# Normalising each score tile in the same step as its maximum, and two fills moved

## The chip, the cores and the metric

The kernel runs on one core of a Trainium2 chip. The metric is device microseconds of one execution. The engines of the core are named as in the profile: PE is TensorE (PEld its weight loads), DVE is VectorE, ACT is ScalarE, POOL is GpSimd and SP is SyncE, which issues most transfers. Every engine runs its own list of instructions in the order in which the program wrote them, and engines wait for each other only through semaphores.

## The reference

The input is `x` of shape (4, 512, 256) and a context of shape (4, 512, 512). Four blocks follow each other, each added to `x` with a gate:

```
x = x + tanh(g_xattn[0]) * L0_xattn(layernorm(x), ctx)   # 16 heads, 1024 keys
x = x + tanh(g_ffn[0])   * L0_ffn(layernorm(x))
x = x + tanh(g_xattn[1]) * L1_xattn(layernorm(x), ctx)   # 16 heads of 64, 512 keys + 1 null key
x = x + tanh(g_ffn[1])   * L1_ffn(layernorm(x))          # 8 experts, top 2
```

The change is in the third block. For each batch and each head it computes, in float32,

```
sim  = (q * scale) @ k.T          # k has a null key in front of its 512 keys
attn = softmax(sim); out = attn @ v
out  = layernorm(out @ Wout) * ln_scale + ln_bias
```

The fourth block starts with a router (logits of 8 experts, the best two, their softmax), whose work for the first batches is interleaved with the third block.

## The kernel before, in words

`layer1` computes the third block. It walks over 32 groups: group `i` is one batch `b` (0 to 3) and one pair of heads `p` (0 to 7), `b, p = divmod(i, 8)`. A group has four steps, `r` = 0 to 3, written out by hand for each engine. The work is staged by one group: in step `r` of group `i`, the scores of query tile `r` (128 queries, two heads of 512 keys, one PSUM bank each) are made for group `i + 1`, while for group `i` the probabilities of key tile `r` are transposed and multiplied with the values.

What each engine writes for a step is this.

- PE: `scores(i + 1, r)` into one of two sets of two banks (so it waits until the exponentials of two tiles ago are done, semaphore `exp_done`), the fill at `(i, r, 0)`, in step 2 the second half of the key projection, `transpose_probs(i, r)` (step 0 waits for `p_ready`, that all four tiles of group `i` are normalised; the others wait for `pT_ready`, that ACT has copied the tile transposed before), the fill at `(i, r, 1)`, and `weigh_values` of the key tile before.
- ACT: `exponentials(i + 1, r)` (two exponentials with a sum each), the read of the fill at `(i, r, 0)`, `keep_probs(i, r)` (the copy of the transposed probabilities), the read of the fill at `(i, r, 1)`, in step 0 `keep_result`, and router work.
- DVE: `maxima(i + 1, r)` (row maximum L1911 and its negative L1913), in step 2 the read of the key projection (L1966), `normalize` (L1919, L1921 and two L1925), `extra` (layer norms and router work at fixed places, a list in `extra`), and its reads of fills.

A fill is some other PE work that uses the one PSUM bank `MISC`: the query projection of group `i + 2` at `(i, 0, 0)`, its key projection at `(i, 1, 0)`, value projections, transposed tokens (`xT`), the null key's scores, the output projection, and the router's transposes (`rT`), `logits` and `prefix` (counts of the chosen experts). The dictionary `slots` gives each its place `(i, r, y)`, with `y` = 0 ahead of the transposes and 1 behind them. Because all share one bank, each fill waits until the one before it has been read, by ACT (`misc_act`) or, for `k`, `null`, `logits`, `prefix` and the second half of `xT`, by DVE (`misc_dve`).

In the kernel before, DVE normalises one step late: in step `r` it normalises tile `r - 1`, and in step 3 tiles 2 and 3.

## Time and profile before

| | us |
|---|---|
| median of 3 executions | 1899.43 (1893.98 to 1903.69) |
| the profiled execution, its own time | 1893.98 |
| its span, first to last instruction | 1892.2 |
| PE busy | 1758.5 (93%) |
| DVE busy | 1215.5 (64%) |
| ACT busy | 1116.9 (59%) |
| POOL busy | 460.0 (24%) |
| mean granted PE clock | 0.986 of full speed |

The span is cut by the program's blocks: the first two blocks of the reference run up to 680 us, `layer1` from 680 to 1447 us, and the experts from there to the end. The shares of busy time are means over these stages. A time in the rows below is counted from the span's start.

### The profile page before, as it was taken

The numbers are of one execution on the slowest core, as the hardware profiler recorded it, in microseconds if no ns is written. First come the engines' busy times: TensorE is split into PE (matmuls) and PEld (weight loads), VectorE is DVE, ScalarE is ACT, GpSimd is POOL, SyncE is SP. The second block draws the span as 40 slices with busy tenths as digits, with TensorE's granted clock in tenths as the row PEclk, the third lists the DMA queues.
The fourth block names the chain that finished last, engine by engine and source line by source line (L and its number), as shares of the span: only waits on it lengthen the run. The fifth ranks groups of instructions, "written<-read, shape, count | busy, mean of one in ns | idle before, by whom it ended". The sixth has DMA issues, their size and how long they took to land. (4 is left out here: it accounts for less than half of the span.)

```text
span 1892.2 us, 28143 instructions
## 1 busy us (share of the span) xinstructions
PE 1758.5 (93%) x9516; PEld 1109.3 (59%) x9516; DVE 1215.5 (64%) x2860; ACT 1116.9 (59%) x2332; POOL 460.0 (24%) x434
## 2 busy tenths in 40 slices
PE   5899997998899999999999999999988989999997
PEld 3555554555454444444544454445436989999997
DVE  4877776876777565455456455645755886666664
ACT  2466666666667556555455545554553666776674
POOL 3010110110110110000010002000204587777775
PEclk9899999999999999999999999999998999999999
DMA  3000000010003066000000000100007568667760
GB/s 101 1 23 1 1 23 1 1 29 0 1 1 134 1 207 200 22 1 1 1 9 15 1 1 24 34 1 12 18 7 245 159 197 229 191 194 223 197 197 6
DMA packets 123054, 128.12 MB, mean 68 GB/s; under 512 B 10912, under 2 KB 118304, under 8 KB 122912
## 3 DMA queue, kind: packets, MB, share of 16 engines
q1 hardware_dynamic: 114176, 117.65, 19.8%
q0 software_dynamic: 8160, 8.67, 2.5%
q8 instruction: 77, 1.26, 0.3%
q14 instruction: 65, 0.53, 0.1%
q10 hardware_dynamic: 576, 0.00, 0.0%
HBM read 97.43 MB, written 30.69 MB: 68 GB/s over the span
## 5 line engine op out<-in xcount | busy, mean ns | idle before, releaser
L1155 DVE TENSOR_REDUCE l_tile_max<-psum 128x1 f32<-128x512 f32 x512 | 342.0, 688 | 105.8 <-PE psum L833 104.3
L1911 DVE TENSOR_REDUCE l_row_max<-psum 128x2 f32<-128x1024 f32 x124 | 151.8, 1224 | 254.1 <-PE psum L1566 253.5
L1003 ACT ACTIVATE l_probs<-psum 128x1024 f32<-128x1024 f32 x256 | 248.2, 1021 | 106.8 <-PE psum L845 103.3
L2578 POOL TENSOR_TENSOR moe_w_lo<-moe_w,moe_w_hi 128x512 fp32r<-128x512 f32 x184 | 259.5, 1411 | 116.9 <-ACT moe_w_hi L2360 115.2
L833 PE MATMUL psum<-l_kT,l_qT 128*128 128x512 f32 x512 | 237.1, 471 | 40.5 <-DVE l_tile_max L1155 37.2
L1752 ACT ACTIVATE l_null_p<-l_s_null,l_neg_max 128x1 f32<-128x1 f32 x248 | 71.6, 289 | 276.9 <-DVE l_neg_max L1913 273.6
L2290 PE MATMUL psum<-moe_xs_hi,moe_w_hi 128*128 128x256 f32 x736 | 212.1, 288 | 2.0 <-DVE moe_xs_lo L2410 2.0
L2290 PE MATMUL psum<-moe_xs_lo,moe_w_hi 128*128 128x256 f32 x736 | 209.7, 285 | 0.0
L2290 PE MATMUL psum<-moe_xs_hi,moe_w_lo 128*128 128x256 f32 x736 | 209.5, 285 | 0.0
L833 PEld LDWEIGHTS psum<-l_kT,l_qT 128*128 128x128 f32 x512 | 98.1, 192 | 131.6 <-DVE l_tile_max L1155 111.1
L1754 ACT ACTIVATE l_probs<-psum,l_neg_max 128x512 f32<-128x512 f32 x248 | 166.6, 672 | 0.0
L845 PE MATMUL psum<-l_qT,l_kT 128*128 128x512 f32 x512 | 161.3, 399 | 1.5 <-ACT l_probs L1003 1.5
L1697 PEld LDWEIGHTS psum<-ident,l_probs 128*128 128x128 f32 x1024 | 119.7, 142 | 71.2 <-issue 59.4
L2558 DVE TENSOR_TENSOR psum<-psum,moe_gate 128x256 f32<-128x256 f32 x184 | 78.8, 428 | 112.9 <-ACT moe_gate L2390 112.8
L2390 ACT ACTIVATE moe_gate<-psum 128x256 f32<-128x256 f32 x184 | 70.9, 385 | 135.6 <-PE psum L2290 134.9
L2290 PEld LDWEIGHTS psum<-moe_xs_hi,moe_w_hi 128*128 128x128 f32 x736 | 142.8, 194 | 2.2 <-DVE moe_xs_lo L2410 2.2
L2290 PEld LDWEIGHTS psum<-moe_xs_lo,moe_w_hi 128*128 128x128 f32 x736 | 142.9, 194 | 0.0
L2290 PEld LDWEIGHTS psum<-moe_xs_hi,moe_w_lo 128*128 128x128 f32 x736 | 142.7, 194 | 0.0
L1566 PE MATMUL psum<-l_qk 64*128 64x512 f32 x496 | 140.9, 645 | 1.2 <-PEq L774 1.2
L860 PE MATMUL psum<-l_probs,l_v_ones 128*32 128x512 f32 x1024 | 139.0, 615 | 0.6 <-ACT l_probs L1003 0.6
L1711 PE MATMUL psum<-l_probsT,l_v_sb 128*64 128x512 f32 x512 | 139.1, 622 | 0.0
L1697 PE MATMUL psum<-ident,l_probs 128*128 128x128 f32 x1024 | 134.7, 275 | 4.2 <-DVE l_probs L1925 3.0
(323 smaller groups left out, 3284.8 us busy)
## 6 DMA issues: line engine op xcount, KB each, us to landing
moe_w<-in_moe_w SPq DMA_DIRECT2D x276, 256.0 KB, 4.7
moe_sorted_x<-l_zeros SPq DMA_DIRECT2D x1, 17680.0 KB, 56.1
moe_xs<-moe_sorted_x SPq DMA_DIRECT2D x23, 272.0 KB
moe_w<-in_ctx SPq DMA_DIRECT2D x8, 512.0 KB, 3.5
moe_w<-in_ctxT SPq DMA_DIRECT2D x4, 1024.0 KB, 5.8
moe_w<-in_wkv SPq DMA_DIRECT2D x2, 2048.0 KB, 15.5
x_resid<-in_x SPq DMA_DIRECT2D x4, 512.0 KB, 10.1
out_x<-x_resid SPq DMA_DIRECT2D x4, 512.0 KB
```

What stands on the lines that cost most here:

```text
L833: nc.tensor.matmul(bank(max_bank(m)), qT[:, q % SLOTS, h, t * P:(t + 1) * P], kT[:, q % SLOTS, h // 2, half * BANK:(half + 1) * BANK], sta ...
L845: last = nc.tensor.matmul(bank(2 * (n % 2) + i), kT[:, q % SLOTS, c, kt * P:(kt + 1) * P], qT[:, q % SLOTS, 2 * c + i, :], start=True, sto ...
L860: last = nc.tensor.matmul(bank(O_BANK)[32 * j:32 * j + 32, :], v_ones[:, q % SLOTS, kt, j, :], probs[:, (n + j // 2) % PT_RING, j % 2, :], ...
L1003: nc.scalar.activation(probs[:, n % PT_RING], wide(2 * (n % 2)), ACT.Exp, scale=SCALE).then_inc(exp_done, 1)
L1155: nc.vector.reduce_max(tile_max[:, q % 2, t, h, half:half + 1], bank(max_bank(m)), AX_X).then_inc(max_read, 1)
L1566: last = nc.tensor.matmul(bank(2 * (t % 2) + j), q_sb[head, i % 2, t * P:(t + 1) * P], k_sb[head, i % 2, :], start=True, stop=True)
L1697: last = nc.tensor.transpose(bank(4 + j)[:, t * P:(t + 1) * P], probs[i % 2][:, t, j, kt * P:(kt + 1) * P], ident[:])
L1711: last = nc.tensor.matmul(bank(O_BANK)[j * DH:(j + 1) * DH, :], v_sb[:, kt, h * DH:(h + 1) * DH], probsT[:, m % 2, j, :], start=(kt == 0), ...
L1754: last = nc.scalar.activation(probs[i % 2][:, t, j, :], bank(2 * (t % 2) + j), ACT.Exp, bias=neg_max[:, t, j:j + 1], scale=SCALE, accum_ou ...
L1911: nc.vector.reduce_max(row_max[:, t, :], wide(2 * (t % 2)).rearrange("p (j m) -> p j m", j=2), AX_X)
L2290: last = nc.tensor.matmul(up_bank(k)[:, n * ROWS:(n + 1) * ROWS], w, x_part[:, i % 2, c, :], start=(c == 0 and j == 0), stop=(c == s.DC - ...
L2578: nc.gpsimd.tensor_tensor(w13_lo[:, k % SPLITS], w13[:, slot_k, :, cols], w13_hi[:, k % SPLITS].bitcast(F32), ALU.subtract).then_inc(w13_s ...
```

## The change

```diff
@@ slots, for batch b + 1 < 4, pair p == 5
-            slots.update({(i, 2, 1): ("xT", b + 1, 0), (i, 3, 0): ("xT", b + 1, 1)})
+            slots.update({(i, 2, 1): ("xT", b + 1, 0), (i, 3, 1): ("xT", b + 1, 1)})
@@ slots of the router, for the routed batches c = 0 and 1
-            at = (first, 2, 1), (first + 1, 0, 1), (first + 2, 2, 1), (first + 4, 0, 1)
+            at = (first, 2, 1), (first + 1, 0, 1), (first + 2, 2, 1), (first + 4, 2, 1)
@@ DVE's step
                         if r == 2:
                             read_fill((i, 1, 0))
-                        if i + 1 < GROUPS and r >= 1:
-                            normalize(i + 1, r - 1)
                         extra(*divmod(i, PAIRS), r)
-                        if i + 1 < GROUPS and r == 3:
+                        if i + 1 < GROUPS:
                             normalize(i + 1, r)
                         if r != 1:
                             read_fill((i, r, 0))
                         read_fill((i, r, 1))
```

There are three edits. DVE now normalises tile `r` in step `r`, behind `extra` and ahead of its reads of fills. The second half of the transposed tokens (`xT`, pair 5 of batches 0 to 2) goes from ahead of the transposes of step 3 to behind them. The router's `prefix` of the first two routed batches (pair 3 of batches 2 and 3) goes from step 0 to step 2. Apart from the order and the waits that hang on it, the instructions are the same. Lines of the changed kernel behind this place are two lower (L2290 is L2288).

On DVE, a plain pair of heads early in the block (batch 0, pair 0, steps 2 and 3) had these rows before, where `l_denom`, `l_recip` and `l_probs` are `normalize` and `l_row_max`, `l_neg_max` are `maxima`:

```order
L1911 TENSOR_REDUCE l_row_max<-psum 128x2 [waits l1_s_psum]
L1913 SCALAR_TENSOR_TENSOR l_neg_max<-l_row_max,l_s_null 128x2
L1919 TENSOR_TENSOR l_denom<-l_p_sum,l_null_p 128x2 [waits l1_exp_done]
L1921 RECIPROCAL l_recip<-l_denom 128x2
L1925 TENSOR_SCALAR l_probs<-l_probs,l_recip 128x512 x2
L1919 TENSOR_TENSOR l_denom<-l_p_sum,l_null_p 128x2 [waits l1_exp_done]
L1921 RECIPROCAL l_recip<-l_denom 128x2
L1925 TENSOR_SCALAR l_probs<-l_probs,l_recip 128x512 x2
L1911 TENSOR_REDUCE l_row_max<-psum 128x2 [waits l1_s_psum]
L1913 SCALAR_TENSOR_TENSOR l_neg_max<-l_row_max,l_s_null 128x2
```

and now has these:

```order
L1911 TENSOR_REDUCE l_row_max<-psum 128x2 [waits l1_s_psum]
L1913 SCALAR_TENSOR_TENSOR l_neg_max<-l_row_max,l_s_null 128x2
L1919 TENSOR_TENSOR l_denom<-l_p_sum,l_null_p 128x2 [waits l1_exp_done]
L1921 RECIPROCAL l_recip<-l_denom 128x2
L1925 TENSOR_SCALAR l_probs<-l_probs,l_recip 128x512 x2
L1911 TENSOR_REDUCE l_row_max<-psum 128x2 [waits l1_s_psum]
L1913 SCALAR_TENSOR_TENSOR l_neg_max<-l_row_max,l_s_null 128x2
```

The pattern of maxima and normalisation is now the same in all four steps, and the wait for `exp_done` ahead of the next `maxima` is for the tile whose maximum was just taken.

On PE, at pair 3 of batch 3, step 2 had these rows before (`l_qk` scores, L1582 the key projection, L1697 the transposes, L1711 the values, L1588 the value projection of step 3), with the `prefix` ahead of all of them in step 0:

```order
L1566 MATMUL psum<-l_qk 128x512 [waits l1_exp_done]
L1582 MATMUL psum<-moe_w 128x512 x2
L1697 MATMUL psum<-ident,l_probs 128x128 [waits l1_pT_ready]
L1711 MATMUL psum<-l_probsT,l_v_sb 64x512 [waits l1_pT_ready]
L1566 MATMUL psum<-l_qk 128x512 [waits l1_exp_done]
L1588 MATMUL psum<-moe_w 128x512 [waits l1_misc_read_dve]
```

and now, with only the first row of each kind shown as above:

```order
L1566 MATMUL psum<-l_qk 128x512 [waits l1_exp_done]
L1582 MATMUL psum<-moe_w 128x512 x2
L1697 MATMUL psum<-ident,l_probs 128x128 [waits l1_pT_ready]
L1645 MATMUL psum<-router_either,router_lower 128x32 [waits l1_zeroed,l1_either_ready,l1_misc_read_dve]
L1646 MATMUL psum<-router_either,router_ones 128x32
L1711 MATMUL psum<-l_probsT,l_v_sb 64x512 [waits l1_pT_ready]
L1566 MATMUL psum<-l_qk 128x512 [waits l1_exp_done]
L1588 MATMUL psum<-moe_w 128x512 [waits l1_misc_read_dve]
```

The `prefix` (L1645, L1646) stands right ahead of the value projection L1588, one block of scores and values between them, and L1588 now waits for DVE's read of the `prefix`; before, that wait was for the read of the keys.

On DVE, at pair 6 of batch 3 (steps 0 and 1, `router_either` the end of the expert ranking) the rows before were:

```order
L498 TENSOR_SCALAR router_either<-router_rank 128x32
L1911 TENSOR_REDUCE l_row_max<-psum 128x2 [waits l1_s_psum]
L1913 SCALAR_TENSOR_TENSOR l_neg_max<-l_row_max,l_s_null 128x2
L1919 TENSOR_TENSOR l_denom<-l_p_sum,l_null_p 128x2 [waits l1_exp_done]
L1921 RECIPROCAL l_recip<-l_denom 128x2
L1925 TENSOR_SCALAR l_probs<-l_probs,l_recip 128x512 x2
L502 TENSOR_TENSOR router_work<-router_chosen,router_logits 128x32
```

and now are:

```order
L498 TENSOR_SCALAR router_either<-router_rank 128x32
L1919 TENSOR_TENSOR l_denom<-l_p_sum,l_null_p 128x2 [waits l1_exp_done]
L1921 RECIPROCAL l_recip<-l_denom 128x2
L1925 TENSOR_SCALAR l_probs<-l_probs,l_recip 128x512 x2
L1911 TENSOR_REDUCE l_row_max<-psum 128x2 [waits l1_s_psum]
L1913 SCALAR_TENSOR_TENSOR l_neg_max<-l_row_max,l_s_null 128x2
L502 TENSOR_TENSOR router_work<-router_chosen,router_logits 128x32
```

The normalisation of tile 0 stands ahead of the maximum of tile 1.

## Rows read from the trace of the kernel before

**Rows 1.** layer1: us; busy of PE, PEld, DVE, ACT, POOL; PEclk, DMA share, GB/s.

```profile
680.00:1447.00 767.00, 742.28 (x3092) 359.31 (x3092) 415.30 (x1137) 411.98 (x1015) 48.96 (x72) 0.99 0.14 44
```

**Rows 2.** Waits of PE, then of DVE: total us, times, longest us.

```profile
PE psum L1573 <- DVE l_rows L1968: 6.7, 3, 2.4
PE psum L1645 <- ACT l_qk L1769: 2.2, 2, 1.1
...
DVE l_row_max L1911 <- PE psum L1566: 253.5, 106, 6.4
DVE l_denom L1919 <- ACT l_probs L1754: 12.2, 20, 0.6
```

**Rows 3.** Timeline, batch 0, pairs 2 to 3: start us, duration us, engine, line.

```profile
733.74 1.13 PE L1566 MATMUL psum<-l_qk 64*128 64x512 f32 x4
736.83 1.13 PE L1566 MATMUL psum<-l_qk 64*128 64x512 f32 x4
741.70 1.13 PE L1566 MATMUL psum<-l_qk 64*128 64x512 f32 x4
...
734.91 1.22 DVE L1911 TENSOR_REDUCE l_row_max<-psum 128x2 f32<-128x1024 f32 x1 [0.99 <-PE psum L1566]
738.03 0.19 ACT L1754 ACTIVATION_READ_ACCUMULATOR l_probs<-psum,l_neg_max 128x1 f32 x1
738.25 0.16 DVE L1919 TENSOR_TENSOR l_denom<-l_p_sum,l_null_p 128x2 f32<-128x2 f32 x1 [0.61 <-ACT l_probs L1754]
739.53 1.22 DVE L1911 TENSOR_REDUCE l_row_max<-psum 128x2 f32<-128x1024 f32 x1
```

**Rows 4.** Timeline of batch 3, pair 3, steps 0 and 2 to 3.

```profile
1327.74 0.41 PE L1645 MATMUL psum<-router_either,router_lower 128*128 128x32 f32 x2 [1.11 <-ACT l_qk L1769]
1328.31 1.08 PE L1711 MATMUL psum<-l_probsT,l_v_sb 128*64 128x512 f32 x4
1328.48 0.87 DVE L521 TENSOR_TENSOR router_run<-router_run,psum 128x8 f32<-128x8 f32 x4 [1.63 <-PE psum L1646]
1337.86 0.15 DVE L1919 TENSOR_TENSOR l_denom<-l_p_sum,l_null_p 128x2 f32<-128x2 f32 x1
1339.30 0.16 DVE L86 TENSOR_TENSOR l_out_work<-l_out_work 128x4 f32<-128x4 f32 x1
1340.09 3.70 PE L1588 MATMUL psum<-moe_w 128*128 128x512 f32 x8
1342.10 1.22 DVE L1911 TENSOR_REDUCE l_row_max<-psum 128x2 f32<-128x1024 f32 x1
1345.93 1.56 PE L1588 MATMUL psum<-moe_w 128*128 128x512 f32 x3 [1.27 <-ACT l_v_sb L1774]
```

**Rows 5.** Timeline, query projections behind the tokens' second half: batches 1 and 2.

```profile
1000.18 1.98 PE L1573 MATMUL psum<-l_rows,moe_w 128*128 128x512 f32 x4 [2.44 <-DVE l_rows L1968]
...
1195.03 0.19 ACT L1754 ACTIVATION_READ_ACCUMULATOR l_probs<-psum,l_neg_max 128x1 f32 x1
1195.83 0.15 DVE L1919 TENSOR_TENSOR l_denom<-l_p_sum,l_null_p 128x2 f32<-128x2 f32 x1
1197.84 3.48 PE L1573 MATMUL psum<-l_rows,moe_w 128*128 128x512 f32 x4 [2.44 <-DVE l_rows L1968]
```

**Rows 6.** PE in stretches around waits: us, PE busy, PEclk, DMA share, GB/s.

```profile
1198.00:1202.00 4.00, 4.00 (x12) 0.64 0.02 4
1002.00:1006.00 4.00, 4.00 (x19) 1.00 0.00 0
```

**Rows 7.** Timeline of batch 3, pair 6, the last exponentials.

```profile
1405.56 1.22 DVE L1911 TENSOR_REDUCE l_row_max<-psum 128x2 f32<-128x1024 f32 x1
1409.82 1.09 PE L1697 MATMUL psum<-ident,l_probs 128*128 128x128 f32 x8 [0.50 <-ACT l_probsT L1792]
1417.15 0.19 ACT L1754 ACTIVATION_READ_ACCUMULATOR l_probs<-psum,l_neg_max 128x1 f32 x1
1418.79 1.48 PE L1697 MATMUL psum<-ident,l_probs 128*128 128x128 f32 x8 [3.04 <-DVE l_probs L1925]
```

## The prediction

> **What bounds the kernel now.** I read the stages first, then each engine's waits, then the timeline at the places where PE waits. In layer1, from 680 to 1447 us, PE is busy 742.3 of 767.0 us at 0.99 of its full clock [rows 1], so the block can give at most 25 us whatever DVE does, and less, since some of those 25 us hang on other things. DVE is busy 415 us of it. Then the waits: PE's for DVE and ACT are short and few; the ones that the change touches are 6.7 us in three waits for DVE's read of the transposed tokens (L1968), 2.2 us in two waits ahead of the prefix [rows 2], and 3.04 us once, near the end, for the normalised probabilities [rows 7]. DVE for its part waits 253.5 us in 106 waits for PE's scores, and only 12.2 us in 20 waits for the exponentials [rows 2]. So PE paces the block, and DVE's order matters only where it makes PE late.
>
> **Edit 1, normalising in the same step: the ring.** It removes no instruction. It makes DVE wait for the exponentials of tile r before it may take the maximum of tile r+1, in steps 0 to 2 of 31 groups (93 waits that were covered by the step's delay). Queued behind each wait are the four instructions of the normalisation, DVE's reads of fills at steps 0, 2 and 3, and the next maximum; ACT waits for that maximum, and behind ACT's exponentials stand its copies, for which PE waits. This makes a ring: maximum, exponentials, normalisation, next maximum. The trace has the ring already, in step 3, where DVE normalised tile 3 at once: the maximum starts at 734.91, ACT's last piece ends at 738.03 + 0.19 = 738.22, DVE goes on at 738.25, and the next maximum starts at 739.53 [rows 3]. That is 4.62 us a turn. PE's step with a query or key projection in it, from one start of the scores to the next, is 741.70 - 736.83 = 4.87 us [rows 3], and most steps of the block are as long or longer, so DVE should wait 0.2 us for the scores in such a step in place of some 2 us, and PE should not notice. The 253.5 us of DVE's wait for scores go mostly to the row for the exponentials. PE is guarded a second time: a late maximum delays PE only through ACT's copy of the transposed tile, and through the scores two tiles on, which come 5 us later.
>
> Where the ring shows all the same is behind a step without a projection (736.83 - 733.74 = 3.1 us [rows 3]), where the maximum was already late: it starts at 739.53, while the scores that started at 736.83 end at 736.83 + 1.13 = 737.96, 1.6 us sooner [rows 3]. There are three such places, all in batch 0: the opening step, pair 0 to 1 and pair 2 to 3. In the opening the second maximum comes 1.2 us late and recovers 0.2 us a step; the copy ahead of the step 3 transposes is then about 0.2 us late. Term: +0.2 us.
>
> Work in extra (layer norm, router) used to come on top of the normalisation and now fits into the wait for the exponentials. DVE gains there, PE does not, save in edit 2.
>
> **Edit 2, the transposed tokens.** The wait for L1968 ends with DVE's normalisation of tile 3, not with PE's transposes, so moving these behind the other transposes should cost and bring nothing by itself. But the normalisation of tile 2 is no longer in that step. In batches 1 and 2 it had pushed that of tile 3 back: DVE began at 1195.83 [rows 5], while the exponentials ended at 1195.03 + 0.19 = 1195.22 [rows 5]. Without it DVE begins at 1195.25. So two of the three waits fall from 2.44 to about 1.87 us, the size of the third (6.7 - 2 x 2.44 = 1.8). Term: -1.15 us.
>
> **Edit 3, the prefix.** It stood behind the query projection in the same bank and waited 1.11 us for ACT, twice [rows 2, 4]; this goes: -2.2 us. In step 2 it follows the key read, which is done. But the value projection L1588 of step 3 then waits until DVE has read the prefix, and DVE reads it behind extra and the new normalisation. In batch 3: DVE is free at 1337.86 (key read done) [rows 4]; the nine small instructions and two scalings of the layer norm took 1339.30 to 1342.10 = 2.8 us [rows 4], so they end at 1340.7; the normalisation takes 739.53 - 738.25 = 1.28 us [rows 3] to 1342.0; the read takes 0.87 + 0.25 us by L521 and the instruction behind it [rows 4], so to 1343.2. PE would reach L1588 at 1340.09 plus the prefix's own 0.57 us (1328.31 - 1327.74) = 1340.66 [rows 4]. It waits about 2.5 us. In batch 2 the two scalings are not in that step: 1.9 us. Against this, the next value projection waited 1.27 us in batch 3 for ACT [rows 4] and 0.62 us in batch 2, since the maximum of step 3 was late (1342.10); with PE itself held back, the late maximum is covered and these waits go. Net: 2.5 + 1.9 - 2.2 - 1.3 - 0.6 = +0.3 us. Bounds: -2.2 us if DVE is in time after all, +4.4 us if none of the removed waits counts.
>
> **The last groups.** In pair 6 of batch 3 DVE has router work in every step, and its maxima are late already: step 1's starts at 1405.56, right behind the ranking of experts [rows 7]. There the normalisation now stands ahead of it: 1405.56 + 1.3 = 1406.86. ACT's exponentials end 3.3 us later (738.22 - 734.91 [rows 3]) at 1410.2, its copy at 1411.2, and PE's transposes, which began at 1409.82 after a 0.50 us wait, begin at 1411.2. Step 2's maximum starts at 1411.5, step 3's at 1411.5 + 4.6 = 1416.1. ACT's row scaling still lies between, so the last exponentials end at 1419.4 against 1417.34 [rows 7], and the last normalisation lets PE go at 1420.85 against 1418.79. Term: +2.1 us. The slot numbers and scaled rows for the scatter, and the list with which SP starts the expert weights, follow the same instructions and shift as much, so nothing behind gives it back. Bounds: 0 and +3 us.
>
> **Sum.** 0.2 - 1.15 + 0.3 + 2.1 = +1.5 us on the profiled execution, 1893.98 us (its span is 1892.2). This execution is the fastest of the three; the median is 1899.43, 5.4 us above. I forecast against the median: 1899.4 + 1.5 = 1901 us.
>
> **The clock.** A wait of 2.44 us was followed once by a stretch at 0.64 of the full clock, between the two levels of 1.2 and 2.4 GHz, in which four query matmuls took 3.48 us in place of 1.98, and once, just as long, by none [rows 5, 6]. So each wait of 2 to 3 us is a coin with 1.5 us on it for 2 us of matmuls. Two of them shrink (batch 2's may keep its clock, -1.5), one of 2.5 us is new ahead of 3.70 us of value projection (up to +3.7).
> The Trainium skill, "TensorE: Matmul & The Clock Gate", Part 1, says that the hardware looks at activity in windows that run freely of the program. By that rule the same wait may or may not cost, as here; the trace agrees, with 1.00 behind one wait of 2.44 us and 0.64 behind the other.
>
> **Rivals.**
> - Gain (1897.5 us): the waits for DVE shrink, the slow stretch of batch 2 goes, and the last groups lose nothing because DVE's extra work there covers the wait. 0.2 - 1.15 - 1.5 + 0.3 = -2.1. For it: DVE has fewer instructions in step 3. Against: in the last groups DVE's start row [rows 7] shows no idle time to give.
> - Slower, the ring longer than PE's step: if a turn costs 5.3 us in place of 4.62, each step of 4.87 us loses 0.43, three in a row 1.3. Of this 0.4 us is slack: ACT's copy takes about 1.1 us behind its exponentials, so it ends 3.3 + 1.1 = 4.4 us after the maximum starts, and PE's transposes of step 3, where no fill stands ahead of them, come 4.87 - 1.17 + 1.1 = 4.8 us after it (1.17 from the scores' start to the maximum: 734.91 - 733.74 [rows 3]). In the dozen groups without that fill PE loses 0.9 us each, +11 us, 1911 us. It decides from a turn of about 5.2 us (0.8 us a group). For it: no step 0 to 2 of the trace shows the ring closed, and the margin is 0.2 us. Against: 20 waits in step 3 all look alike (12.2 / 20 = 0.61 us) [rows 2], with 0.03 us from ACT's end to DVE's start.
> The Trainium skill, same page, "Architectural detail", says that ScalarE and VectorE take their queues strictly in order. By it a waiting normalisation holds the next maximum even where the scores are ready; the trace agrees: DVE waits until 738.25, and the maximum of scores that ended at 737.96 starts at 739.53. It is this rival's reason, and the 0.2 us are its margin.
> - Clock (1905 us): the new wait ahead of the value projection is followed by a slow stretch, 1.5 + 3.7 = +5.2 us.
> - The last groups' 2.1 us double, since ACT is held by the row scaling too: +3.6, 1903 us; inside the range.
>
> **Chances.** Forecast within 2 us of its sum 0.58, gain 0.14, clock and last groups 0.16, ring 0.12. About 0.5%, 9.5 us, is what a measurement of this kernel can tell from no change. Only the ring reaches it, and run noise (the three times spread over 9.7 us): faster 0.04, same 0.85, slower 0.11. The range reaches from the gain to the threshold: 1895 to 1909 us.
>
> **What would show it.** Right: DVE's wait for scores falls from 253 us to well under 100, and that for the exponentials rises from 12 to over 100; the steps of 4.87 us stay; L1573's three waits are all near 1.9 us; L1645's ACT wait is gone and L1588 waits for DVE about 2 us twice; the transposes of the last pair start some 2 us later. Wrong: PE waits for copies (L1697 for ACT) in ordinary groups, which is the ring, or a step with a projection longer than 4.87 us where no PE wait stood before.

## The result and the profile after

| | before | after |
|---|---|---|
| median beside each other (8 runs each) | 1900.35 us | 1911.67 us (1900.76 to 1917.78) |
| ratio, 95% interval | | 1.0055 [1.003, 1.0082] |
| span of the profiled execution | 1892.2 us | 1904.4 us |
| mean granted PE clock | 0.986 | 0.983 |

The changed kernel is slower by 0.55%, and its median lies above the range of 1895 to 1909 us. Compared twice more on later occasions it gave 1.0019 [1.0002, 1.0037] and 1.0028 [1.0011, 1.0045]. The three together are about 1.0034, that is +6.5 us. So the cost is real; the later two put it at +3.6 and +5.3 us, the first at +10.5 us.

The two profiled executions differ by 12.2 us of span. To divide that, I cut both at two marks: the first scores of layer1 (L1566), and the last pair's transposes (L1697, the row with the wait of about 3 us for the probabilities [rows 7]). The stretch between them is called layer1's stretch below.

| us | before | after | difference |
|---|---|---|---|
| up to the first scores | 680.23 | 685.96 | +5.7 |
| layer1's stretch | 738.56 | 744.37 | +5.8 |
| from there to the end | 473.4 | 474.1 | +0.7 |

The first 5.7 us lie in code that the change doesn't touch. In other profiled executions of the same changed kernel the first scores start at 681.45 and 685.87 us. So the 5.7 us are not the change's. Its own cost is layer1's stretch: +5.8 us. In two further executions of the changed kernel the same stretch grew by 6.3 and 8.6 us (e10 and e5 below), so one execution's stretch holds to some 3 us; what the change costs is therefore read place by place.

What answers to [rows 1] is this stretch of the changed kernel, with the same columns:

```profile
686.00:1459.00 773.00, 745.14 (x3092) 360.38 (x3092) 423.04 (x1137) 411.60 (x1015) 48.62 (x72) 0.99 0.14 44
```

PE has the same 3092 instructions; it is busy 2.9 us longer and idle 3.1 us longer (773.00 - 745.14 = 27.9 against 24.7 us). So half of the cost is waits, and half is the same matmuls taking longer.

The waits, to be held against [rows 2]:

```profile
DVE l_row_max L1911 <- PE psum L1566: 136.4, 78, 7.9
DVE l_denom L1919 <- ACT l_probs L1754: 133.6, 103, 1.9
...
PE psum L1573 <- DVE l_rows L1968: 5.6, 3, 1.9
PE psum L1588 <- DVE router_work L524: 5.6, 2, 3.4
PE psum L1697 <- ACT l_probsT L1792: 3.2, 2, 1.8
```

About half of DVE's idle time moved from the scores to the exponentials, and PE hardly notices: there is no new PE wait in ordinary groups. The wait for scores did not fall to "well under 100" us, as the prediction had it, but to 136.4. The block's 123 steps from one block of scores to the next take 731.6 us, 5.95 us on the mean, and a turn of 4.62 us leaves 1.3 us of each. New are the two waits of L1588 for DVE's read of the prefix, 5.6 us together. Two waits for ACT's copies in the last pair but one grew from 1.2 to 3.2 us together.

The plain steps of batch 0, pairs 2 to 3, where [rows 3] stand, read now:

```profile
734.78 1.13 PE L1566 MATMUL psum<-l_qk 64*128 64x512 f32 x4
739.64 1.13 PE L1566 MATMUL psum<-l_qk 64*128 64x512 f32 x4
742.73 1.13 PE L1566 MATMUL psum<-l_qk 64*128 64x512 f32 x4
...
740.81 1.22 DVE L1911 TENSOR_REDUCE l_row_max<-psum 128x2 f32<-128x1024 f32 x1 [0.16 <-PE psum L1566]
744.15 0.16 DVE L1919 TENSOR_TENSOR l_denom<-l_p_sum,l_null_p 128x2 f32<-128x2 f32 x1 [1.88 <-ACT l_probs L1754]
745.43 1.22 DVE L1911 TENSOR_REDUCE l_row_max<-psum 128x2 f32<-128x1024 f32 x1
```

Here the ring is closed in every step. A turn is 745.43 - 740.81 = 4.62 us, PE's step with a projection is still 739.64 - 734.78 = 4.86 us, and DVE waits just 0.16 us for scores. A step without projection (3.09 us) makes the next maximum late, and PE loses nothing.

The place of the prefix in batch 3, to be held against [rows 4]:

```profile
1341.36 0.16 DVE L86 TENSOR_TENSOR l_out_work<-l_out_work 128x4 f32<-128x4 f32 x1
1343.50 0.73 DVE L154 TENSOR_SCALAR l_rows<-l_rows,l_out_mv,l_out_work 128x256 f32<-128x256 f32 x2
1343.99 1.50 POOL L1853 TENSOR_TENSOR l_rows<-l_rows,l_ln_scale 128x256 f32<-128x256 f32 x2 [150.06 <-DVE l_rows L154]
1344.15 0.68 DVE L1919 TENSOR_TENSOR l_denom<-l_p_sum,l_null_p 128x2 f32<-128x2 f32 x1
1345.15 1.02 DVE L1925 TENSOR_SCALAR l_probs<-l_probs,l_recip 128x512 f32<-128x512 f32 x2
1346.27 0.88 DVE L521 TENSOR_TENSOR router_run<-router_run,psum 128x8 f32<-128x8 f32 x4
1347.22 0.19 DVE L524 TENSOR_TENSOR router_work<-router_run,psum 128x32 f32<-128x32 f32 x1
1347.46 6.55 PE L1588 MATMUL psum<-moe_w 128*128 128x512 f32 x8 [3.44 <-DVE router_work L524]
```

DVE has no idle moment from the layer norm to the read at 1347.22. PE waits 3.44 us, and then its eight value matmuls take 6.55 us where they took 3.70 [rows 4]. The stretches of this place (the two of batch 2 first) show why. Columns are us, then busy of PE, PEld, DVE, ACT and POOL, then PEclk:

```profile
1147.00:1151.00 4.00, 3.72 (x6) 1.68 (x7) 2.51 (x8) 1.81 (x6) 1.51 (x2) 0.68 0.00 0
1151.00:1155.00 4.00, 4.00 (x15) 2.14 (x14) 0.83 (x2) 1.62 (x2) 0.00 (x0) 0.90 0.00 0
1347.00:1351.00 4.00, 3.54 (x4) 1.51 (x5) 3.29 (x9) 1.81 (x6) 1.82 (x2) 0.50 0.01 2
1351.00:1355.00 4.00, 4.00 (x14) 2.25 (x13) 1.43 (x4) 0.68 (x2) 0.62 (x3) 0.72 0.00 0
```

The granted clock is 0.50 behind the wait of batch 3, which is the lower level of 1.2 GHz, and 0.68 behind the wait of 2.12 us in batch 2, where the value matmuls take 5.40 us.

Each place of the sum, from one mark to the next in both traces:

| us | forecast | measured |
|---|---|---|
| opening, up to pair 1 | +0.2 | +0.2 |
| transposed tokens, batches 1 and 2 | -1.15 | -0.57 - 2.06 = -2.6 |
| prefix, batches 2 and 3 | +0.3 | +1.88 + 3.69 = +5.6 |
| router's logits, pair 5 of batch 3 | none | +0.6 |
| last pair | +2.1 | 19.50 to 21.50, +2.0 |
| sum | +1.5 | +5.8 of 5.8 |

### The profile page after: what moved, and what is told of

It is laid out like the page before. It is cut to its first block and busy times, and to the rows that moved or that the text cites. A ratio compares the mean times of both kernels' runs of the same rounds, so it can differ in the third digit from the quotient of the medians.

```text
span 1904.4 us, 28143 instructions
## 1 busy us (share of the span) xinstructions
PE 1764.4 (93%) x9516; PEld 1111.8 (58%) x9516; DVE 1223.9 (64%) x2860; ACT 1115.9 (59%) x2332; POOL 459.3 (24%) x434
## 5 line engine op out<-in xcount | busy, mean ns | idle before, releaser
L1911 DVE TENSOR_REDUCE l_row_max<-psum 128x2 f32<-128x1024 f32 x124 | 151.6, 1223 | 137.5 <-PE psum L1566 136.4
L2288 PE MATMUL psum<-moe_xs_hi,moe_w_hi 128*128 128x256 f32 x736 | 211.5, 287 | 1.4 <-DVE moe_xs_lo L2408 1.4
L2288 PE MATMUL psum<-moe_xs_lo,moe_w_hi 128*128 128x256 f32 x736 | 209.2, 284 | 0.0
L2288 PE MATMUL psum<-moe_xs_hi,moe_w_lo 128*128 128x256 f32 x736 | 209.0, 284 | 0.0
L1697 PEld LDWEIGHTS psum<-ident,l_probs 128*128 128x128 f32 x1024 | 119.3, 142 | 75.2 <-issue 59.2
L2288 PEld LDWEIGHTS psum<-moe_xs_hi,moe_w_hi 128*128 128x128 f32 x736 | 142.2, 193 | 1.7 <-DVE moe_xs_lo L2408 1.7
L2288 PEld LDWEIGHTS psum<-moe_xs_lo,moe_w_hi 128*128 128x128 f32 x736 | 142.3, 193 | 0.0
L2288 PEld LDWEIGHTS psum<-moe_xs_hi,moe_w_lo 128*128 128x128 f32 x736 | 142.2, 193 | 0.0
L1566 PE MATMUL psum<-l_qk 64*128 64x512 f32 x496 | 140.9, 645 | 1.2 <-PEq L774 1.2
L1697 PE MATMUL psum<-ident,l_probs 128*128 128x128 f32 x1024 | 134.8, 275 | 6.2 <-ACT l_probsT L1792 3.2
L1711 PE MATMUL psum<-l_probsT,l_v_sb 128*64 128x512 f32 x512 | 139.1, 622 | 0.0
```

The lines of the kernel that those rows point to most:

```text
L1566: last = nc.tensor.matmul(bank(2 * (t % 2) + j), q_sb[head, i % 2, t * P:(t + 1) * P], k_sb[head, i % 2, :], start=True, stop=True)
L1697: last = nc.tensor.transpose(bank(4 + j)[:, t * P:(t + 1) * P], probs[i % 2][:, t, j, kt * P:(kt + 1) * P], ident[:])
L1711: last = nc.tensor.matmul(bank(O_BANK)[j * DH:(j + 1) * DH, :], v_sb[:, kt, h * DH:(h + 1) * DH], probsT[:, m % 2, j, :], start=(kt == 0), ...
L1911: nc.vector.reduce_max(row_max[:, t, :], wide(2 * (t % 2)).rearrange("p (j m) -> p j m", j=2), AX_X)
L2288: last = nc.tensor.matmul(up_bank(k)[:, n * ROWS:(n + 1) * ROWS], w, x_part[:, i % 2, c, :], start=(c == 0 and j == 0), stop=(c == s.DC - ...
```

## Experiments

The table gives, for all twelve, the ratio to the kernel before on the same chip, and layer1's stretch in the profiled execution (before: 738.56 us).

| kernel | ratio [95%] | layer1's stretch |
|---|---|---|
| e1, edit 1 alone | 0.9995 [0.9978, 1.0012] | 741.3 (+2.8) |
| e2, edit 3 alone | 1.0025 [1.001, 1.004] | 742.9 (+4.3) |
| e3, edits 1 and 2 | 0.9999 [0.9981, 1.0017] | 741.5 (+3.0) |
| e4, edit 2 alone | 1.0006 [0.9987, 1.0025] | 738.6 (+0.1) |
| e5, changed kernel again | 1.0019 [1.0002, 1.0037] | 747.1 (+8.6) |
| e6, prefix read first | 1.0013 [0.9996, 1.0029] | 741.8 (+3.2) |
| e7, changed, 2 multiplications more | 1.0338 [1.0318, 1.0357] | 804.5 (+65.9) |
| e8, before, 2 multiplications more | 1.0112 [1.0093, 1.013] | 761.9 (+23.4) |
| e9, edits 1 and 2, last pair but one in the old order | 1.0013 [0.9996, 1.0031] | 739.5 (+1.0) |
| e10, changed kernel a third time | 1.0028 [1.0011, 1.0045] | 744.8 (+6.3) |
| e11, changed, GpSimd's multiplication small | one execution | 744.8 (+6.2) |
| e12, changed, 1 multiplication more | 1.0146 [1.012, 1.0173] | 766.2 (+27.6) |

### One edit at a time

e1 has the new order of `normalize` alone:

```diff
-                        if i + 1 < GROUPS and r >= 1:
-                            normalize(i + 1, r - 1)
                         extra(*divmod(i, PAIRS), r)
-                        if i + 1 < GROUPS and r == 3:
+                        if i + 1 < GROUPS:
                             normalize(i + 1, r)
```

> Edit 1 alone: DVE normalises each tile in its own step; both fills stay where they were. Theory A (the step-by-step account: the ring of 4.62 us fits into PE's steps, only the last groups are late): PE's steps of 4.86 us stay, the transposes of the last pair come 2 us later, the token waits shrink to 1.87 us, no wait of L1588 for DVE; layer1 about +1 us, time between -2 and +3 us of before. Theory B (the ring is what made the changed kernel slower by 11 us): the whole loss is here, +8 to +12 us.

e2 has the move of the prefix alone:

```diff
-            at = (first, 2, 1), (first + 1, 0, 1), (first + 2, 2, 1), (first + 4, 0, 1)
+            at = (first, 2, 1), (first + 1, 0, 1), (first + 2, 2, 1), (first + 4, 2, 1)
```

> Edit 3 alone, with the old order of the normalisation: the router's prefix in step 2 of pair 3. Theory A (the prefix is late because of the layer norm work in front of DVE's read of it, and each wait is followed by slow matmuls): L1588 waits 2.1 and about 3 us for DVE, both followed by value projections of 5.4 to 6.5 us in place of 3.7; +5 to +6 us. Theory B (the new normalisation, which waits for the exponentials, is what holds the read back): no wait over 1 us here, -2 us.

e3 is the changed kernel with that line put back:

```diff
-            at = (first, 2, 1), (first + 1, 0, 1), (first + 2, 2, 1), (first + 4, 2, 1)
+            at = (first, 2, 1), (first + 1, 0, 1), (first + 2, 2, 1), (first + 4, 0, 1)
```

> The changed kernel without edit 3 (prefix back in step 0; edits 1 and 2 stay). Theory A: the two long waits of L1588 and their slow stretches are gone, the waits of 1.1 us of L1645 are back, the last groups still 2 us late: about 5.6 us faster than the changed kernel, 0 to +2 us against before. Theory B (ring): as slow as the changed kernel, +9 to +11 us.

e4 has the move of the tokens' second half alone:

```diff
-            slots.update({(i, 2, 1): ("xT", b + 1, 0), (i, 3, 0): ("xT", b + 1, 1)})
+            slots.update({(i, 2, 1): ("xT", b + 1, 0), (i, 3, 1): ("xT", b + 1, 1)})
```

> Edit 2 alone: the second half of the transposed tokens behind the transposes of step 3, old order of the normalisation. Theory A: nothing depends on it, waits of L1573 stay 1.9, 2.4 and 2.4 us, 0 us within 2 us. Rival: the move alone gives the gain of the token waits, -1 to -3 us.

Only the move of the prefix is outside no change by its interval: 1.0025 alone, and without it the rest is 0.9999. In e2's trace L1588 waits for DVE 2.00 us in batch 2 and 2.77 us in batch 3, and both times the value matmuls behind it took 5.40 us. The stretches of batch 3 show the clock. Their columns are us, PE busy, PEclk, DMA share, GB/s:

```profile
1341.00:1345.00 4.00, 1.23 (x7) 1.00 0.00 0
1345.00:1349.00 4.00, 4.00 (x6) 0.57 0.01 2
1349.00:1353.00 4.00, 4.00 (x17) 1.00 0.00 0
```

Here the prefix waits with the old order of normalising in place. So its cost comes from where the prefix stands, behind `extra` on DVE, and not only from the new order. The waits give 2.00 + 2.77 less the removed 1.11 + 1.11 + 0.62 + 1.27 = +0.7 us, the slow matmuls 2 x 1.70 = +3.4 us; together 4.1 us. From mark to mark the two places grow by 1.8 us each, 3.6 of the +4.3 us of the stretch, a little under the 5 to 6 us that I expected.

In e3 I expected the stretch to be 5.6 us shorter than the changed kernel's. It is 2.9 us shorter. The two places of the prefix give back 4.9 us, since L1588's wait for ACT in batch 3 is 1.95 us there; but the query projection behind the tokens of batch 2 is slow again, 3.38 us where the changed kernel has 1.98.

e1 and e4 separate the tokens. With edit 2 alone the three waits are 1.88, 2.45 and 2.44 us, as before. With edit 1 alone they are 1.87 us each. The shortening belongs to edit 1, by the mechanism that the prediction gave; edit 2 by itself does nothing. What the clock does behind that wait in batch 2 hangs on edit 3 as well. The changed kernel first, then e1:

```profile
1204.40 1.98 PE L1573 MATMUL psum<-l_rows,moe_w 128*128 128x512 f32 x4 [1.87 <-DVE l_rows L1968]
1198.16 3.22 PE L1573 MATMUL psum<-l_rows,moe_w 128*128 128x512 f32 x4 [1.87 <-DVE l_rows L1968]
```

With the new order and the prefix in step 2 the four matmuls took 1.98 us in all five executions (the changed kernel three times, e6, e11); with the prefix in step 0 they took 3.22 to 3.38 us in all three (e1, e3, e9), behind the same wait. So edit 3 costs 5.6 us in its own places and gives 1.7 us back here, from mark to mark. Why it does is open.

e1's +2.8 us of the stretch is hardly seen in its time: the interval of 0.9978 to 1.0012 ends at +2.3 us. e1's rows of pair 6 of batch 3 and of the mark behind it show its cost:

```profile
1413.28 1.08 PE L1697 MATMUL psum<-ident,l_probs 128*128 128x128 f32 x6 [1.77 <-ACT l_probsT L1792]
1422.97 1.09 PE L1697 MATMUL psum<-ident,l_probs 128*128 128x128 f32 x8 [2.92 <-DVE l_probs L1925]
```

The wait of 1.77 us was 0.50 us before [rows 7]. It is there in every kernel with the new order in that pair (1.77 in e3, 1.76 in e6), and in none with the old (0.50 in e2 and e4).

### The changed kernel twice more

e5 and e10 are the changed kernel itself.

> The changed kernel once more, beside the same executions of the kernel before as the next three. Theory A (layer1 6 us longer, the rest of the first 11 us is the spread between executions): ratio 1.002 to 1.0045, and both value projections behind the prefix slow again. Theory B (a cost of 11 us that the trace of layer1 does not show): 1.005 or more again.

> The changed kernel once more, on another occasion, since its first two comparisons gave ratios of 1.0055 and 1.0019. If layer1's +5.8 us in the traces is all that the change costs, the ratio is 1.003 (+5 to +6 us), and both earlier intervals are one value measured with more scatter than they say. Rival: the first comparison was the right one and the change costs 10 us: 1.0055.

The ratios are 1.0019 and 1.0028. The first comparison's interval begins at 1.003, so the three meet near +6 us, which is what layer1's stretch gives. The place of the prefix is the same every time; e5, batches 2 and 3:

```profile
1142.73 5.40 PE L1588 MATMUL psum<-moe_w 128*128 128x512 f32 x8 [2.12 <-DVE router_work L524]
1342.88 2.07 PE L1588 MATMUL psum<-moe_w 128*128 128x512 f32 x2 [3.44 <-DVE router_work L524]
```

The waits are equal to 0.01 us in all three executions, and the matmuls behind each are slow: the eight take 5.40 us in batch 2 each time, and 6.60 us in e5 and 6.53 us in e10 in batch 3 (the second row above has the first two of e5's eight). What differs lies elsewhere. e5 has a wait of 2.28 us ahead of a value projection of pair 4 (L1588 for ACT) where the first execution has 0.77 us; ACT itself is idle for 1.41 us ahead of that copy, and the trace names no engine of the core for it. In pair 5 the logits' matmuls (L1639) took 2.75 us in place of 1.92. These two places are the whole difference of 2.8 us. And the experts' part took 478.5 us behind the last mark, against 474.1. I have no cause for any of the three.

### The read ahead of the other work

e6 lets DVE read the prefix ahead of `extra` and `normalize`:

```diff
+                        early = slots.get((i, r, 1), ("",))[0] == "prefix"
+                        if early:
+                            read_fill((i, r, 1))
                         extra(*divmod(i, PAIRS), r)
...
-                        read_fill((i, r, 1))
+                        if not early:
+                            read_fill((i, r, 1))
```

> The changed kernel with DVE's read of the prefix ahead of the layer norm work and the normalisation, in step 2 of pair 3 of batches 2 and 3. Theory A (the read stands behind too much DVE work): L1588 no longer waits for DVE's read of the prefix. But the maximum of step 3 stays as late, so the next value projection waits for ACT instead, 1.3 us in batch 2 and 2.5 us in batch 3; about 1.7 us of waits less, and up to 4.5 us of slow matmuls less if the shorter waits keep the clock: -2 to -6 us against the changed kernel. Rival (the prefix is late on PE itself): waits of L1588 for DVE stay over 1.5 us.

The wait for DVE is gone from L1588, and a wait for ACT stands in its place one projection later. The rows of batch 3, and the stretches around them with busy of PE, PEld, DVE, ACT and POOL ahead of the clock:

```profile
1342.47 3.70 PE L1588 MATMUL psum<-moe_w 128*128 128x512 f32 x8
1346.55 1.21 DVE L1911 TENSOR_REDUCE l_row_max<-psum 128x2 f32<-128x1024 f32 x1
1349.75 0.59 ACT L1774 ACTIVATE l_v_sb<-psum 128x512 f32<-128x512 f32 x1
1350.39 3.70 PE L1588 MATMUL psum<-moe_w 128*128 128x512 f32 x8 [3.34 <-ACT l_v_sb L1774]
```

```profile
1347.00:1351.00 4.00, 0.66 (x3) 0.38 (x3) 3.21 (x9) 2.96 (x8) 2.44 (x4) 1.00 0.01 2
1351.00:1355.00 4.00, 4.00 (x12) 1.26 (x10) 0.80 (x2) 0.85 (x2) 0.00 (x0) 1.00 0.00 0
```

The layer norm and the normalisation take DVE until 1346.55 in any case; the maximum of step 3 is late, ACT's exponentials behind it, and behind those ACT's read of the first value projection (1349.75), on which the second waits. The two waits sum to 2.01 + 3.34 = 5.35 us against 2.12 + 3.44 = 5.56. So reading early moves the wait and doesn't remove it; I had expected waits for ACT of 1.3 and 2.5 us, 1.7 us less in all. In batch 2 the matmuls behind the wait take 5.40 us as before, and the place costs as much as in the changed kernel. But behind the 3.34 us of batch 3 the clock stays at 1.00, and that place costs 2.8 us less from mark to mark, the 2.85 us of its slow value matmuls; the stretch is 744.4 - 741.8 = 2.6 us shorter. This divides the two costs on the chip: nearly the same waits, without one of the slow stretches.

### GpSimd beside the normalisation

e11 reduces GpSimd's multiplication by `ln_scale` to four of 256 columns (the output's scale is left out for the others):

```diff
-                        nc.gpsimd.tensor_tensor(rows[:, t, :], rows[:, t, :], ln_scale[:], ALU.mult).then_inc(scaled, 1)
+                        nc.gpsimd.tensor_tensor(rows[:, t, 0:4], rows[:, t, 0:4], ln_scale[:, 0:4], ALU.mult).then_inc(scaled, 1)
```

> The changed kernel, with GpSimd's multiplication by ln_scale (L1853) reduced to the first four columns of 256 (the output's scale is left out for the rest). If that multiplication beside DVE's normalisation is what made the wait of batch 3 longer than predicted, L1588's wait for DVE there falls from 3.44 us to 2.5 to 2.8, with L1919 at 0.16 us and L1925 at 0.88. Rival: the layer norm's own instructions are longer in the chain than I summed; then it stays at 3.2 to 3.5. The wait of batch 2 stays at 2.12 either way.

```profile
1342.35 0.52 POOL L1853 TENSOR_TENSOR l_rows<-l_rows,l_ln_scale 128x4 f32<-128x4 f32 x2 [150.06 <-DVE l_rows L154]
1342.51 0.15 DVE L1919 TENSOR_TENSOR l_denom<-l_p_sum,l_null_p 128x2 f32<-128x2 f32 x1
1342.98 0.88 DVE L1925 TENSOR_SCALAR l_probs<-l_probs,l_recip 128x512 f32<-128x512 f32 x2
1345.15 2.08 PE L1588 MATMUL psum<-moe_w 128*128 128x512 f32 x2 [2.77 <-DVE router_work L524]
```

The wait falls from 3.44 to 2.77 us, L1919 from 0.68 to 0.15 us and L1925 from 1.02 to 0.88 us (0.53 + 0.14 = 0.67 us, all of the difference). The multiplication is the cause. The other 0.27 us over the forecast's 2.5 stay: the chain of layer norm, normalisation and read as summed was that much short. This place is 2.1 us shorter than in the changed kernel (its eight value matmuls take 5.09 us, not 6.55). The stretch did not get shorter (744.8 us), since pair 4 is 0.9 us longer (a wait of 1.65 us ahead of its value projection) and pair 5 2.1 us longer (the logits' matmuls take 3.55 us, not 1.92). I have no cause for these two; it is one execution.

### How near the ring is

e7 adds two multiplications by 1.0 behind each normalisation in the changed kernel, e8 the same in the kernel before, e12 one of them in the changed kernel:

```diff
+                    dve.drain()
+                    for j in range(2):
+                        part = probs[i % 2][:, t, j, :]
+                        last = nc.vector.tensor_scalar(part, part, 1.0, None, ALU.mult)
```

(e12 has `range(1, 2)` in the second line.)

> The changed kernel with each normalisation followed by a second multiplication of the same tiles by 1.0 (0.9 us more of DVE each, no change of values). Theory A (the ring has 0.25 us to spare): a turn is now 5.5 us against PE's 4.86, PE waits for ACT's copy (L1697) in the groups without a fill ahead of the last transposes, +12 to +25 us against the changed kernel. Rival (PE is far from the ring): less than 5 us.

> The kernel before with the same second multiplication. Theory A: the normalisation is off the ring in steps 0 to 2, where DVE waits over 2 us for scores; only the step without a projection, the token waits and the last groups pay: +5 to +10 us against before, much less than the same addition costs the changed kernel. Rival (DVE's busy time itself counts): as much as in the changed kernel.

> The changed kernel with one more multiplication by 1.0, of one head's probabilities, behind each normalisation. With two of them the ring's turn went from 4.61 to 5.44 us and layer1 lost 0.58 us (5.44 - 4.86) in most of its 124 steps. With one the turn is about 5.03: if the margin is the difference of turn and step, 0.25 us, it loses 0.17 us a step, 15 to 22 us over the changed kernel. Rival: the copy's slack of 0.4 us counts, as the prediction had it (decides at 5.2 us), and it loses under 5 us.

e7, steps behind each other in batch 0:

```profile
743.01 1.22 DVE L1911 TENSOR_REDUCE l_row_max<-psum 128x2 f32<-128x1024 f32 x1
748.46 1.21 DVE L1911 TENSOR_REDUCE l_row_max<-psum 128x2 f32<-128x1024 f32 x1
753.90 1.22 DVE L1911 TENSOR_REDUCE l_row_max<-psum 128x2 f32<-128x1024 f32 x1
747.28 1.09 PE L1697 MATMUL psum<-ident,l_probs 128*128 128x128 f32 x8 [1.54 <-ACT l_probsT L1792]
754.04 1.09 PE L1697 MATMUL psum<-ident,l_probs 128*128 128x128 f32 x8 [1.69 <-DVE l_probs L1929]
```

e12, the same places:

```profile
740.89 1.22 DVE L1911 TENSOR_REDUCE l_row_max<-psum 128x2 f32<-128x1024 f32 x1
746.00 1.22 DVE L1911 TENSOR_REDUCE l_row_max<-psum 128x2 f32<-128x1024 f32 x1
740.05 1.09 PE L1697 MATMUL psum<-ident,l_probs 128*128 128x128 f32 x8 [0.87 <-ACT l_probsT L1792]
746.14 1.09 PE L1697 MATMUL psum<-ident,l_probs 128*128 128x128 f32 x8 [1.02 <-DVE l_probs L1929]
```

A turn is 5.44 us in e7 and 5.11 us in e12; there is no idle time ahead of a maximum, and PE waits for ACT's copies in plain groups, which is what the prediction named as the sign of the ring. The stretch grows over the changed kernel's 744.4 us by 60.1 us at a turn of 5.44 and by 21.8 us at 5.11.

Not all of that is the ring: the tokens, the prefix and pairs 4 to 7 of batch 3 grow too. Without these places, counted from one block of scores to the next, e7 loses 40.6 us, in 29 steps that are over 0.4 us longer than the changed kernel's, and e12 12.4 us, in 14 such steps. An estimate from these two: the line through them reaches zero at a turn of 5.11 - 12.4 x 0.33 / 28.2 = 4.96 us, just above PE's step of 4.86.

My expectation of e7 (12 to 25 us) was far too low. The loss stands in one or two steps of a group, as I had it, but not only in groups without a fill: PE also waits for ACT's read of a fill (L1588 for ACT, 12.8 us in seven waits in e7), and a single step loses up to 3.2 us. The expectation of e12 (15 to 22 us at a turn of 5.03) held partly by luck: the turn was 5.11, and a loss in most of 124 steps, as it says, did not occur.

In e8 the same work costs 23.4 us, also above the 5 to 10 us that I expected: in step 3 two normalisations stand in a row, so each place where PE waits for the last of them grows: the tokens' waits of batches 1 and 2 from 2.44 to 4.79 us, the last pair's from 3.04 to 5.54, and two plain groups wait 0.77 us where there was no wait. Both long ones of the tokens were followed by query matmuls of 3.78 us, where the kernel before has 1.98 and 3.48. Outside the places named above e8 loses 4.9 us, against e7's 40.6: that difference is what the new order makes of the same work.

### A version without both losses

e9 puts the prefix back into step 0 and gives the last pair but one the old order of DVE:

```diff
-            at = (first, 2, 1), (first + 1, 0, 1), (first + 2, 2, 1), (first + 4, 2, 1)
+            at = (first, 2, 1), (first + 1, 0, 1), (first + 2, 2, 1), (first + 4, 0, 1)
...
+                        late = i == GROUPS - 2
+                        if late and r >= 1:
+                            normalize(i + 1, r - 1)
                         extra(*divmod(i, PAIRS), r)
-                        if i + 1 < GROUPS:
+                        if i + 1 < GROUPS and (not late or r == 3):
                             normalize(i + 1, r)
```

> The changed kernel with the prefix back in step 0 and, for the last pair but one alone, DVE's old order of normalising. What is left is the shorter wait for the transposed tokens. If the loss sits in the prefix place (+5.6 us in the profile) and in the last groups (+2 us), both are gone: L1588 waits for ACT about 1.3 us in batch 3 and not for DVE, the last pair's transposes wait about 3.0 us as in the kernel before, and layer1 takes 738.6 - 0.6 = about 738 us against 738.56. Time: 0 to -3 us against the kernel before. Rival: the same-step order costs something of its own everywhere; then it stays 2 us or more above.

Both losses are gone in its trace: no wait of L1588 for DVE, and the last pair's transposes as before. What remains is a wait for ACT in batch 3 that was 1.27 us [rows 4]:

```profile
1349.97 3.70 PE L1588 MATMUL psum<-moe_w 128*128 128x512 f32 x8 [1.95 <-ACT l_v_sb L1774]
```

It is 0.7 us longer, as in e1 and e3 (1.95 each), since DVE's maximum stands behind layer norm and normalisation there. From mark to mark the tokens give 0.9 us, while this wait takes 0.7, pair 4 0.3, pairs 5 and 6 0.9 and the opening 0.2 us. The stretch is 739.5 us, +1.0 and not the -0.6 us that I expected; the time is 1.0013 [0.9996, 1.0031]: no change, and no gain over the kernel before. By its time alone the rival, +2 us or more, is not excluded.

## Why the prediction was wrong

The mechanism of each step was as predicted, and one term was mis-sized: **edit 3, the prefix**, "Net: 2.5 + 1.9 - 2.2 - 1.3 - 0.6 = +0.3 us". It measured +5.6 us.

- **The removed waits** went as said: 1.11 twice, 0.62 and 1.27 us.
- **The new waits** were 3.44 and 2.12 us in place of 2.5 and 1.9, +1.2 us. 0.67 us of it is GpSimd's multiplication beside the normalisation (e11). The kernel before had shown this in the same batch, in a normalisation that started beside that multiplication; I read the durations of quiet places and did not look at what runs on GpSimd just then. Its rows:

```profile
1345.22 2.20 POOL L1853 TENSOR_TENSOR l_rows<-l_rows,l_ln_scale 128x256 f32<-128x256 f32 x2 [1.77 <-DVE l_rows L154]
1346.05 0.70 DVE L1919 TENSOR_TENSOR l_denom<-l_p_sum,l_null_p 128x2 f32<-128x2 f32 x1
```

- **The clock** was the larger part. The prediction called the slow stretch behind a wait a coin, gave it nothing in the sum, and put it in a rival of its own, "1.5 + 3.7 = +5.2 us". It cost 1.70 us behind the wait of batch 2 and 2.85 us behind that of batch 3, 4.55 us. (0.3 + 1.2 + 4.55 is 6.0 us; from mark to mark it is 5.6, and the other 0.4 us I can't place.) Seven profiled executions have the prefix in step 2 and its read behind the other work (the changed kernel three times, e2, e7, e11, e12), so 14 such waits, of 2.00 to 4.28 us; slow matmuls, 5.09 to 6.60 us for eight, followed all but one (e12's in batch 2, 2.62 us). The rival was thus what happened. That its size was right is partly luck: it had one slow stretch at 3.7 us, and two came, of 1.70 and 2.85 us, beside a gain of 1.5 us at the tokens. It deserved most of the chance, and not 0.16 shared with another. The kernel before could have told: I counted one fall in its two token waits of 2.44 us, but it has two more waits of that size, 2.48 us ahead of the logits (1396.24) and 3.04 us ahead of the last pair (1418.79), and the clock fell behind both, so three times in four. The stretches behind these two, with us, PE busy, PEclk, DMA share, GB/s:

```profile
1399.29:1403.29 4.00, 4.00 (x18) 0.63 0.00 0
1418.79:1422.79 4.00, 4.00 (x16) 0.57 0.09 35
```

The other steps:

- **The ring** (edit 1 in ordinary groups): right, with a turn of 4.62 us and steps of 4.86 us, no cost. Its rival did not occur; that its 1911 us is the first median, 1911.67, is chance, since e1 has the ring and a ratio of 0.9995. Its price was too low as well: it was said to decide at a turn of 5.2 us and to cost 11 us at 5.3, while e12 loses 12.4 us in ordinary steps at 5.11, and the line through e12 and e7 gives an estimate of 29 us at 5.3. The slack of 0.4 us in ACT's copy does not save it, as each late step makes the next one later.
- **The tokens**: the waits are 1.87 to 1.88 us all three, as predicted. In batch 2 the clock stayed up behind the shorter wait as well, 1.98 us in place of 3.48 us, which made -2.6 us of -1.15. That was the gain rival's term, and it came only together with edit 3: in e1, e3 and e9 the clock fell behind the same wait of 1.87 us.
- **The last groups**: +2.0 us, predicted +2.1. Not foreseen was +0.6 us one pair earlier, at the router's logits: their wait is 2.83 us in place of 2.48, and the rest is matmuls behind them at a low clock, which e2 has without the longer wait.
- **The median**: 1899.43 + 5.8 = 1905 us would follow from the stretch alone. The three comparisons put the changed kernel's median 11.3, 2.8 and 5.3 us above that of the kernel before, which itself was 1900.35, 1903.34 and 1905.37 us. So medians move by several us from one occasion to another, and the range gave too little for that: its upper end of 1909 stood only 4 us above the clock rival's 1905. The first comparison's 11.3 us are 5.5 us more than the stretch shows; for these there is no cause, and the later two comparisons don't have them.

The Trainium skill, "TensorE: Matmul & The Clock Gate", Part 1, says that the hardware looks at activity in windows that run freely of the program, and from this I made a coin of equal sides. The trace agrees only in part: behind 1.87 us in batch 2 the clock fell in three kernels and stayed up in three others, and e6's 3.34 us went without a fall; but the five executions of those three others agreed with each other, and the six waits of the changed kernel's prefix in three executions all had the same outcome. A rule that leaves the outcome open says nothing against its coming back each time.

A rule that I had not applied bears on the slower normalisation. The measurement is L1919 at 0.68 us beside the multiplication and 0.15 us without it. The Trainium skill, "SBUF — State Buffer", section "Who interferes with whom", says that contention is on the pair of ports that VectorE and GpSimd share alone, and that "it's an exclusive lock", which the later of the two waits for. The trace agrees: L1919 adds two operands of SBUF, and the GpSimd instruction beside it reads SBUF.

What stays open: why the clock falls in one place each time and in another not, behind waits of the same length; and why the experts' part took 473.4 to 474.1 us in some executions and 478.5 to 482.7 in others.

## What to carry to other kernels

A fill that is moved behind another engine's long list of work costs the wait, and then the matmuls behind it at a clock down to half: price both in the sum, not one of them as a rival. Ahead of a chain of small instructions, look at what the neighbouring engine runs at the same moment. Where a ring turns nearly as slowly as the engine it feeds steps, the slack is little more than the difference of the two (here 0.24 us): the delay adds up from step to step, and the engine pays it in one or two steps of each group.

## What the runs showed of the hardware

- The first scores of layer1, behind code that is the same in all kernels, start between 680.23 and 685.97 us in 14 profiled executions. The changed kernel itself has 681.45 and 685.96, and the stretch from 20 to 40 us shows the granted clock with which they go; first the execution that begins layer1 at 685.96, then e5, which begins it at 681.45:

```profile
20.00:40.00 20.00, 16.21 (x49) 0.74 0.01 1
```

```profile
20.00:40.00 20.00, 15.32 (x63) 1.00 0.03 6
```

  The start goes with this clock: five executions with 1.00 reach the first scores at 681.45 to 681.75 us, three with 0.83 at 684.48 to 684.53 and five with 0.74 at 685.50 to 685.97. It is not all of it, since the kernel before has 0.91 and the earliest start, 680.23.

  The spread is as large as the whole effect of the change; one profiled execution of each kernel can't be subtracted without marks around the changed part.
- A wait of 3.34 us was followed by a granted clock of 1.00 (e6, batch 3), one of 2.00 us by 0.62 (e2, batch 2, 1143 to 1147 us): length alone does not tell. At one place of one program the outcome came back: 1.98 us in five of five executions, 3.22 to 3.38 us in three of three, behind the same wait of 1.87 us.
- An addition of 128x2 elements on DVE takes 0.15 us alone and 0.68 us beside a GpSimd multiplication of 128x256.
